# Four chunks convolved ahead of the expert units, the other stages spread between them

## The chip, the cores and the metric

The kernel runs on one core of one Trainium2 chip. The metric is the device time of one execution in microseconds. Three runs of the kernel before gave 195.55, 196.88 and 197.39 us, median 196.88 us.

## The reference, cut to what matters

The input is 32 images of 64 channels and 16x16 pixels. A first layernorm over channels (LN1) is followed by a blockwise fp4 quantisation, a 3x3 convolution with quantised weights and a residual. Then each pixel is a token of 64 values: a second layernorm (LN2), a gate that picks two of eight experts, and the experts themselves, all eight computed for every token and weighed by the gate (zero for the experts not picked).

```python
x = x + conv(fake_quant(_ln_c(x)), fake_quant(w))        # fake_quant: 16 values share a power-of-two scale
xf = _ln_t(to_tokens(x))
probs = softmax(xf @ gate_w + gate_b);  cw = the top two of probs, zero elsewhere
for e in range(8):
    out += cw[:, e] * (gelu(xf @ W1[e] + b1[e]) @ W2[e] + b2[e])      # 64 -> 128 -> 64
x = x + from_tokens(out)
```

## The kernel before

**Tiles.** The 16 pairs of images lie as [128, 4096]: 2 x 64 channels on the partitions, pixels on the free axis. They are cut into NCH = 8 chunks of W = 512 columns. A chunk is 1024 tokens.

**Stages of a chunk.** LN1: TensorE centres (`center_chunk`, a product with a centring matrix, which also turns the tile), ScalarE squares, VectorE sums (`reduce_squares`), ScalarE takes the root (`deviations`), VectorE inverts and multiplies (`invert`, `normalise`; ScalarE does it for chunks 6 and 7). Quantisation: TensorE turns the chunk back (`transpose_xn`), ScalarE takes the absolute value (`take_v`), VectorE finds the maxima of blocks and rounds by adding and removing a large number (`block_maxima`, `block_bounds`, `block_magics`, `magics`, `bias`), GpSimd writes the result as bf16 into a padded tile (`quantised`). Convolution: nine products of 128x512 (`convolve`), residual (`take_conv` on ScalarE and `residual` on GpSimd, or `residual` on VectorE for chunks 5 to 7). LN2 goes as LN1 (`center_x2`, `square`, `reduce_squares`, `deviations`, `invert`, `normalise`), then the fp32 values are split in two fp16 halves (`high_half`, `low_half`), turned (`transpose_halves`) and copied out of PSUM (`take_xT`). Routing: TensorE makes the logits (`logits`), VectorE shifts them by their maximum (`shifted_logits`), ScalarE takes exponentials, VectorE finds the two largest and their places (`route_max`, `route_index`) and computes the weights (`route_select`, `route_gates`); TensorE turns them (`transpose_gates`), ScalarE copies them (`take_gateT`), and SyncE writes them to DRAM and reads them back spread over all partitions into `gbc` (`spread_gates`, 2 MB a chunk in four transfers, each awaited by the first unit that needs it).

**Expert units.** One chunk times one expert is a unit n = 8c + u; there are 64. `first_product` is eight fp16 matmuls of 128x512 (two halves of W1, two column groups, two image sets) into one of two pairs of PSUM banks; `gelus` is one ScalarE instruction on 128x1024; `second_product` is four fp32 matmuls; `weigh` on VectorE adds the bias and multiplies by the spread gate; `add_unit` on GpSimd adds to x2. `first_product(n)` waits for the gelu of n-2, `second_product(n)` for the gelu of n and the weighing of n-2, `weigh(n)` for the addition of n-4. On TensorE the order is first product of n, second product of n-2.

**Order.** Every engine runs its own queue in program order, written out by hand, and waits on semaphores. In the kernel before, all eight chunks go through LN1, quantisation, convolution, residual and nearly all of LN2 first. Four chunks are turned and have logits, and chunk 0 has its gates, when TensorE issues `ffn(0, first=True)`; the halves and logits of chunks 4 to 7 stand between the units of chunk 0. From chunk 1 on each block of eight units holds only the routing of a later chunk: on VectorE `route_gates(c + 2)` stands after `weigh` of unit 4 of chunk c, on TensorE `transpose_gates(c + 1)` after unit 1 of chunk c. ScalarE, GpSimd, VectorE and SyncE run this part in loops, TensorE unrolled. Exponentials are taken in three lots (`LOGIT_PARTS`), so the Gelu table of ScalarE is loaded twice (L563, L567). The end (L922 to L924): VectorE adds the last unit itself, then the last chunk is stored.

## Time and profile before

| what | value |
|---|---|
| median of three runs | 196.88 us |
| the profiled execution | 198.83 us |
| its span, first to last instruction | 195.9 us |
| TensorE (PE) matmuls busy | 166.7 us, 85% of the span |
| VectorE (DVE) busy | 138.3 us, 71% |
| GpSimd (POOL) busy | 127.9 us, 65% |
| ScalarE (ACT) busy | 116.7 us, 60% |
| mean granted TensorE clock | 0.952 |

The profiled execution lies 1.95 us above the median of the runs, and 2.9 us of it lie outside the span. All times in rows are microseconds from the start of the span unless marked ns. A matmul's end is modelled, and matmuls overlap, so the pace is read from start to start and not from the length of one.

### The profile page before, as it was taken

Reading aid. Unit: us, or ns where it says so; the run is one execution under the profiler, and the core shown is the slowest. Engines: PE = TensorE matmul, PEld = TensorE weight load, DVE = VectorE, ACT = ScalarE, POOL = GpSimd, SP = SyncE. Lnnn points to the kernel's source line nnn. Section 1 sums busy time; section 2 is a strip of 40 time slices with the busy share of each in tenths; the row PEclk is TensorE's granted clock in tenths of the full one; section 3 lists DMA queues with packets and bytes.
Section 4 is the critical chain, followed back from the end, with each engine's and each line's share of the span. In section 5 each row is a group of like instructions: output and inputs, shape, how many; then the busy total and the mean of one; then the engine's idle time right before and its main releaser. Section 6 shows DMA issues by size and latency. Waiting matters only on the chain.

```text
span 195.9 us, 3972 instructions
## 1 busy us (share of the span) xinstructions
PE 166.7 (85%) x1214; PEld 84.6 (43%) x1214; DVE 138.3 (71%) x442; ACT 116.7 (60%) x153; POOL 127.9 (65%) x120
## 2 busy tenths in 40 slices
PE   1986159899773697997999999999999899999980
PEld 1984125465472343542443443444443344444420
DVE  0899999999778985794684784595694395344451
ACT  3276902572488283469776767766776656776630
POOL 7699134799980442457577677577668477588482
PEclk9999859999997579999999999999999999999998
DMA  6990000000000059499089379569469559669601
GB/s 163 326 134 0 3 0 2 3 0 3 0 0 0 10 161 206 77 215 199 17 204 206 83 168 208 117 169 207 116 158 201 133 149 208 136 159 204 172 0 54
DMA packets 16320, 22.39 MB, mean 114 GB/s; under 512 B 2344, under 2 KB 8112, under 8 KB 16304
## 3 DMA queue, kind: packets, MB, share of 16 engines
q1 hardware_dynamic: 16144, 22.04, 50.3%
q8 instruction: 9, 0.15, 0.3%
q10 hardware_dynamic: 160, 0.15, 0.3%
q14 instruction: 7, 0.06, 0.1%
HBM read 19.82 MB, written 2.36 MB: 113 GB/s over the span
## 4 chain that ended last, share of the span: by engine, by line
PE 48%; DVE 25%; DMA 11%; ACT 7%; issue 6%; SPq 1%; POOLq 1%; ACTq 0%; DVEq 0%
PE ps L1060 23%; PE ps L1077 21%; DMA gbc<-gate_rows 6%; DVE xn L721 5%; DVE ssum L629 4%; DVE xn L641 2%; DMA gate_rows<-gateT 2%; DVE gbc L703 2%; DMA cw<-in_conv_w 2%; ACT xn L458 2%; DVE gbc L708 1%; DVE gbc L713 1%; PE ps L1016 1%; ACT hl L504 1%; DVE topi L801 1%
## 5 line engine op out<-in xcount | busy, mean ns | idle before, releaser
L411 POOL TENSOR_TENSOR x<-x,y_sb 128x512 f32 (+1 forms) x63 | 80.3, 1274 | 40.7 <-DVE y_sb L840 36.5
L557 ACT ACTIVATE work<-ps,bias_sb,w_back 128x1024 f32<-128x1024 f32 x64 | 77.0, 1204 | 37.9 <-PE ps L1060 37.7
L840 DVE SCALAR_TENSOR_TENSOR y_sb<-ps,bias_sb,gbc 128x512 f32<-128x512 f32 x64 | 47.4, 746 | 41.4 <-PE ps L1077 29.6
L1077 PE MATMUL ps<-work,w_sb 128*64 128x512 f32 x256 | 65.7, 593 | 1.0 <-DVE y_sb L840 0.9
L1060 PE MATMUL ps<-xT,w_hi 128*64 128x512 f16 x256 | 39.6, 389 | 1.1 <-ACT work L557 1.1
L1060 PE MATMUL ps<-xT,w_lo 128*64 128x512 f16 x256 | 39.3, 387 | 0.0
L1060 PEld LDWEIGHTS ps<-xT,w_hi 128*64 128x64 f16 x256 | 13.7, 111 | 33.3 <-issue 30.5
L1077 PEld LDWEIGHTS ps<-work,w_sb 128*64 128x64 f32 x256 | 17.9, 137 | 14.1 <-issue 2.1
L1060 PEld LDWEIGHTS ps<-xT,w_lo 128*64 128x64 f16 x256 | 15.0, 112 | 13.5 <-issue 1.0
L983 PE MATMUL ps<-qpad,cw_bd 128*128 128x512 bf16 x72 | 19.0, 411 | 1.7 <-POOL qpad L355 1.6
L355 POOL TENSOR_TENSOR qpad<-work,xn 128x512 bf16<-128x512 f32 (+1 forms) x8 | 10.6, 1328 | 8.7 <-DVE work L727 8.7
L390 POOL TENSOR_TENSOR hl<-xn,hl x8 | 9.2, 1160 | 9.1 <-DVE hl L763 9.0
L430 ACT ACTIVATE work<-ps 128x512 f32<-128x512 f32 x16 | 9.5, 594 | 7.4 <-PE ps L936 7.4
L936 PE MATMUL ps<-center,x_sb 128*128 128x128 f32 x64 | 10.1, 336 | 4.1 <-DMA x_sb<-in_x 4.1
L629 DVE TENSOR_REDUCE ssum<-work 128x8 f32<-128x512 f32 x16 | 10.4, 678 | 2.6 <-ACT work L430 2.6
L936 PEld LDWEIGHTS ps<-center,x_sb 128*128 128x128 f32 x64 | 9.9, 251 | 4.0 <-POOL stack_id L323 4.0
L983 PEld LDWEIGHTS ps<-qpad,cw_bd 128*128 128x128 bf16 x72 | 7.0, 102 | 10.2 <-issue 3.6
L451 ACT ACTIVATE work<-ps 128x512 f32<-128x512 f32 x8 | 4.6, 633 | 8.6 <-PE ps L950 8.6
L721 DVE SCALAR_TENSOR_TENSOR xn<-work,gbc 128x512 f32<-128x512 f32 x8 | 9.6, 1202 | 0.0
L641 DVE TENSOR_TENSOR xn<-ps,rstd 128x512 f32<-128x512 f32 x14 | 9.2, 681 | 0.1
L936 PE MATMUL ps<-center,x 128*128 128x128 f32 x64 | 8.6, 278 | 0.6 <-POOL x L363 0.6
L936 PEld LDWEIGHTS ps<-center,x 128*128 128x128 f32 x64 | 8.2, 191 | 1.9 <-POOL x L363 1.1
(113 smaller groups left out, 175.8 us busy)
## 6 DMA issues: line engine op xcount, KB each, us to landing
gbc<-gate_rows SPq DMA_DIRECT2D x16, 768.0 KB, 10.1
gbc<-gate_rows SPq DMA_DIRECT2D x16, 256.0 KB, 4.0
x_sb<-in_x SPq DMA_DIRECT2D x8, 256.0 KB, 5.3
out<-x SPq DMA_DIRECT2D x8, 256.0 KB, 10.4
w_raw<-in_W SPq DMA_DIRECT2D x2, 256.0 KB, 6.5
w_sb<-in_W SPq DMA_DIRECT2D x1, 256.0 KB
gate_rows<-gateT SPq DMA_DIRECT2D x8, 32.0 KB, 3.8
cw<-in_conv_w ACTq DMA_DIRECT2D x2, 72.0 KB, 3.9
```

The lines of the kernel that those rows point to most:

```text
L355: pool.tensor_tensor(qpad[:, ds(2 * c, 2), 1:SIDE + 1, 1:SIDE + 1], work[:, ds(c * W, W)].rearrange("p (q h w) -> p q h w", q=2, h=SIDE), ...
L411: pool.tensor_tensor(x2[:, ds(c * W, W)], x2[:, ds(c * W, W)], y_sb[:, u % H_RING, :], ALU.add).then_inc(added, 1)
L430: act.activation(work[:, ds(c * W, W)], bank(c), ACT.Square).then_inc(squared, 1)
L557: act.activation(h_sb[:, u % H_RING, :], bank(H + 2 * (u % 2), 2 * W), ACT.Gelu, bias=b1_sb[:, u:u + 1], scale=w_back[:, u:u + 1]).then_in ...
L629: dve.tensor_reduce(ssum[:, ds(c, 1), :].rearrange("p z g -> p (z g)"), by_group(work[:, ds(c * W, W)]), AX.X, ALU.add).then_inc(summed, 1)
L641: dve.tensor_tensor(by_group(xn[:, ds(c * W, W)]), by_group(bank(c)), wide_groups(rstd, c), ALU.mult).then_inc(ready, 1)
L721: dve.scalar_tensor_tensor(blk(xn[:, ds(c * W, W)]), blk(work[:, ds(c * W, W)]), MAGIC, smallest.to_broadcast([128, BLKS, BLK]), ALU.mult, ...
L840: dve.scalar_tensor_tensor(y_sb[:, u % H_RING, :], bank(Y + u % 2), b2_sb[:, u:u + 1], gbc[:, slot, u, :], ALU.add, ALU.mult).then_inc(wei ...
L936: last = pe.matmul(ps[:, col:col + 128], src[:, col:col + 128], center[:, :], start=True, stop=True)
L983: last = pe.matmul(bank(c), cw_bd[:, k, :, :].rearrange("p r o -> p (r o)"), qpad[:, ds(2 * c, 2), k // 3:k // 3 + SIDE, k % 3:k % 3 + SID ...
L1060: last = pe.matmul(ps[q * CH:(q + 1) * CH, at:at + W], w_half[:, u * HIDDEN + q * CH:u * HIDDEN + (q + 1) * CH], xT[:, ds(c * CTOK + r * W ...
L1077: last = pe.matmul(ps[r * CH:(r + 1) * CH, (Y + u % 2) * W:(Y + u % 2 + 1) * W], w2_sb[:, u, :], h_sb[:, u % H_RING, r * W:(r + 1) * W], s ...
```

## The change

The work of each stage is nearly the same. Its place in the five queues is another.

- **In front** of unit 0 stand: LN1 of all chunks; quantisation, convolution and residual of chunks 0 to 3 (`HEAD = 4`); LN2, halves, turning and logits of chunks 0 and 1; the routing of chunk 0.
- **All else** stands in one loop over s = 0 ... 65 on each engine, unrolled. In step s TensorE issues the first product of unit s, the second product of unit s-2, and then what `due` names: a stage with distance `ahead` is issued for chunk c in step s = 8c - ahead. ScalarE issues the due stages and then the gelu of s, VectorE the due stages and then `weigh(s - 2)`, GpSimd the due stages and then `add_unit(s - 3)`.
- The distances are constants at the top: turning 29, absolute value 28, maxima and bounds 27, magics 26, bias 25, quantised 24, convolution 23, residual 21, centring 17, squares 16, sums 15, root 14, normalise 13, high half 12, low half and turning of halves 11, copy 10, logits 9, shift 8, maxima of logits 7, index and exponentials 6, gates and turning of gates 4, copy of gates 3.
- Banks 0 and 1 of PSUM serve all stages in the loop; each TensorE stage waits until the one before has been read.
- Exponentials are taken per chunk, each followed by a load of the Gelu table. The root of LN2 of chunks 2 to 7 is a power of -0.5 on GpSimd.
- `route_copy` goes. Residual is VectorE's for all chunks, high half ScalarE's for all. The convolution weights are spread by one VectorE and one ScalarE instruction in place of four VectorE ones, and their scale is multiplied into the sign on VectorE in place of a GpSimd step.
- `gbc` is filled in eight transfers of 256 KB a chunk in place of two of 256 KB and two of 768 KB, each part awaited by the unit that first needs it, and each written once the weighing two chunks before is past it.
- `h_sb` is a tile of its own.

```diff
+LN1_PARTS = ((0, 3), (3, 8))
+HEAD = 4
+GATE_PARTS = ((0, 2), (2, 4), (4, 6), (6, 8))
+TURN, ABS, BOUND, MAGN, BIASED, QUANT, CONV, RESID = 29, 28, 27, 26, 25, 24, 23, 21
+CENTRE, SQUARE, SUMS, ROOT, NORM, HIGH, LOW, TURNH, TAKEN, LOGITS = 17, 16, 15, 14, 13, 12, 11, 11, 10, 9
+SHIFT, TOPS, EXPS, INDEX, GATES, TURNG, TAKENG = 8, 7, 6, 6, 4, 4, 3
+        def due(s, ahead):
+            c, rest = divmod(s + ahead, UNITS)
+            return c if rest == 0 and c < NCH else None
...
@@ sync @@
+                    if c >= 2:
+                        sp.wait_ge(weighted, UNITS * (c - 2) + last)
...
+            for c in range(NCH):
+                send_rows(c)
+                spread_gates(c)
+                if c >= 2:
+                    store(c - 2)
...
@@ gpsimd @@
+            quantised(0)
+            quantised(1)
+            pool.wait_ge(w_inv_ready, 1)
+            pool.tensor_tensor(by_expert(w_scaled), by_expert(w_raw), ...
+            quantised(2)
+            pool.wait_ge(w_hi_ready, 1)
             pool.tensor_tensor(w_lo[:, :], w_scaled[:, :], w_hi[:, :], ALU.subtract).then_inc(w_lo_ready, 1)
+            low_half(0)
+            quantised(3)
+            low_half(1)
+            for s in range(SLOTS + 2):
+                for ahead, stage in ((QUANT, quantised), (ROOT, inverse_root), (LOW, low_half)):
+                    c = due(s, ahead)
+                    if c is not None and not (stage is quantised and c < HEAD):
+                        stage(c)
+                if 3 <= s:
+                    add_unit(s - 3)
...
@@ scalar @@
+            deviations2(1)
+            high_half(1)
+            load_table(ACT.Exp)
+            exponentials(0)
+            load_table(ACT.Gelu)
+            take_xT(1)
+            for s in range(SLOTS):
+                for ahead, stage in ((HIGH, high_half), (ABS, take_v), (SQUARE, square2),
+                                     (TAKEN, take_xT), (EXPS, exponentials), (TAKENG, take_gateT)):
+                    c = due(s, ahead)
+                    if c is not None:
+                        stage(c)
+                        if stage is exponentials:
+                            load_table(ACT.Gelu)
+                gelu(s)
+                if s == 0:
+                    take_gateT(0)
...
@@ vector @@
+            reduce1(0)
+            upper_steps()
+            reduce1(1) ... reduce1(3); invert1(0); normalise1(0); reduce1(4); normalise1(1); reduce1(5) ... reduce1(7)
+            bounds(0); invert1(1); normalise1(6); normalise1(7); spread_conv_weights()
+            magics(0); bias(0); take_conv_weights(); normalise1(2); weight_maxima()
+            bounds(1); magics(1); bias(1); weight_exponents(); residual(0); normalise1(3); weight_powers()
+            bounds(2); magics(2); bias(2); reduce2(0); residual(1); invert2(0); normalise2(0)
+            bounds(3); magics(3); bias(3); reduce2(1); residual(2); invert2(1); normalise2(1)
+            shifted_logits(0); settled(); route_max(0); route_index(0); residual(3); route_gates(0)
+            for s in range(SLOTS + 2):
+                for ahead, stage in ((SHIFT, shifted_logits), (SUMS, reduce2), (TOPS, route_max), (INDEX, route_index),
+                                     (NORM, normalise2), (RESID, residual), (GATES, route_gates),
+                                     (BOUND, bounds), (MAGN, magics), (BIASED, bias)):
+                    c = due(s, ahead)
+                    if c is not None and not (stage is residual and c < HEAD):
+                        stage(c)
+                if s == 3:
+                    weigh(0)
+                    weigh(1)
+                if s >= 4:
+                    weigh(s - 2)
...
@@ tensor @@
+            def first_product(n):
+                c, u = divmod(n, UNITS)
+                pe.wait_ge(xT_ready, c + 1)
+                if n < 2:
+                    pe.wait_ge(x2_by_dve, HEAD)
+                    pe.wait_ge(xn1_by_act, len(LN1_ACT))
                 else:
                     pe.wait_ge(gelu_done, n - 1)
...
+            convolve(3)
+            turn_halves(1)
+            centre2(2)
+            logits(1)
+            for s in range(SLOTS + G2_LAG):
+                if s < SLOTS:
+                    first_product(s)
+                if s >= G2_LAG:
+                    second_product(s - G2_LAG)
+                if s == 0:
+                    turn_gates(0)
+                for ahead, stage in ((CONV, convolve), (TURN, turn_chunk), (TURNG, turn_gates), (TURNH, turn_halves),
+                                     (LOGITS, logits), (CENTRE, centre2)):
+                    c = due(s, ahead)
+                    if c is not None and not (stage is convolve and c < HEAD):
+                        stage(c)
```

On VectorE the lines with several calls stand for one call a line. `route_gates(c)` now holds both comparisons of the places, the sum of the exponentials, its reciprocal, the sum of the two selections, the pick and the last product.

## Rows read from the trace of the kernel before

**Rows 1.** Windows: stretch and its length; busy time (instructions) of each engine; clock; DMA

```profile
9.10:57.00 47.90, 37.29 (x239) 25.06 (x238) 46.27 (x89) 25.01 (x62) 35.94 (x30) 0.93 0.12 18
66.00:71.50 5.50, 5.50 (x33) 2.44 (x32) 5.07 (x18) 3.66 (x6) 3.47 (x3) 0.52 0.21 69
106.00:190.00 84.00, 83.01 (x564) 34.64 (x563) 50.58 (x176) 56.42 (x52) 59.53 (x48) 1.00 0.69 155
```

The engines stand in the order PE, PEld, DVE, ACT, POOL.

**Rows 2.** Chain that ended last: start, us, what (L1060 first product, L1077 second)

```profile
66.29 1.85 PE ps L1060 x6
...
77.41 0.55 PE ps L1016 x8
...
78.95 0.86 PE ps L1077 x4
79.81 0.89 PE ps L1029 x32
...
95.40 0.86 PE ps L1060 x8
96.27 0.86 PE ps L1077 x4
...
189.18 1.09 PE ps L1077 x4
...
190.30 0.76 DVE y_sb L840
```

L1016 turns halves, L1029 makes logits (here of two chunks).

**Rows 3.** Timeline of PE: start, us, engine, line (L950 turn, L983 conv, L936 centre)

```profile
33.52 0.60 PE L950 MATMUL ps<-identf,xn 128*128 128x128 f32 x4
33.95 2.19 PE L983 MATMUL ps<-qpad,cw_bd 128*128 128x512 bf16 x9
...
40.86 2.19 PE L983 MATMUL ps<-qpad,cw_bd 128*128 128x512 bf16 x9
42.89 1.05 PE L936 MATMUL ps<-center,x 128*128 128x128 f32 x8
43.77 1.05 PE L983 MATMUL ps<-qpad,cw_bd 128*128 128x512 bf16 x4
```

**Rows 4.** Groups of instructions by line and shape: busy us, mean ns, idle before

```profile
L708 DVE TENSOR_SCALAR gbc<-gbc 128x32 f32<-128x32 f32 x8 | 3.5, 439 | 0.0
...
L504 ACT ACTIVATE hl<-xn 128x512 f16<-128x512 f32 x4 | 2.5, 630 | 2.5 <-DVE xn L641 2.5
...
L511 ACT ACTIVATE xT<-ps 128x1024 f16<-128x1024 f16 x4 | 4.0, 1020 | 0.0
```

**Rows 5.** Timeline in front: sums, two largest logits, then the spreading of chunk 0's gates

```profile
11.20 1.86 DVE L629 TENSOR_REDUCE ssum<-work 128x8 f32<-128x512 f32 x3
...
61.08 0.58 DVE L795 MAX8 top<-lcur 128x8 f32<-128x8 f32 x8
...
66.33 0.27 ACT L526 ACTIVATE gateT<-ps 64x128 f32<-64x128 f32 x1 [2.63 <-PE ps L1045]
...
76.21 0.74 DVE L840 SCALAR_TENSOR_TENSOR y_sb<-ps,bias_sb,gbc 128x512 f32<-128x512 f32 x1
```

**Rows 6.** Timeline of DVE and POOL around the gates of one chunk

```profile
115.63 1.27 POOL L411 TENSOR_TENSOR x<-x,y_sb 128x512 f32 x1 [0.34 <-DVE y_sb L840]
...
115.73 1.25 DVE L823 TENSOR_TENSOR picked<-ex,sel 128x64 f32<-128x64 f32 x1
...
117.02 0.27 DVE L827 TENSOR_TENSOR gate<-picked,rsum 128x64 f32<-128x64 f32 x1
```

**Rows 7.** Timeline around the exponentials of chunks 4 to 7 and the next first product

```profile
87.40 1.28 ACT L518 ACT_TABLE_LOAD   x1
88.69 0.42 ACT L518 ACTIVATE ex<-ex 128x256 f32<-128x256 f32 x1
...
90.53 3.62 ACT L557 ACTIVATE work<-ps,bias_sb,w_back 128x1024 f32<-128x1024 f32 x3
...
91.77 0.62 PE L1060 MATMUL ps<-xT,w_hi 128*64 128x512 f16 x4 [1.11 <-ACT work L557]
```

More of the change, by code:

```diff
@@ new lines, in gelu @@
+            def gelu(n):
+                act.wait_ge(g1_done, n + 1)
+                if n >= H_RING:
+                    act.wait_ge(g2_done, n - H_RING + 1)
+                u = n % UNITS
+                act.activation(h_sb[:, n % H_RING, :], bank(H + 2 * (n % 2), 2 * W), ACT.Gelu,
+                               bias=b1_sb[:, u:u + 1], scale=w_back[:, u:u + 1]).then_inc(gelu_done, 1)
+            act.wait_ge(eps_ready, 1)
+            load_table(ACT.Sqrt)
+            for c in range(5):
+                square1(c)
@@ L652, in _, with reduce1, invert1 @@
-            normalise(3, LN1_PARTS, rstd1, xn1_ready)
-            invert(LN1_PARTS, 1, std1, rstd1)
-            for c in range(4, XN_BY_DVE):
-                normalise(c, LN1_PARTS, rstd1, xn1_ready)
+                return t[:, c, :].unsqueeze(2).to_broadcast([128, GROUPS, CH])
+            def reduce1(c):
+                dve.wait_ge(sq1, c + 1)
+                dve.tensor_reduce(ssum[:, c, :], by_group(chunk(work, c)), AX.X, ALU.add).then_inc(ss1, 1)
+            def invert1(k):
+                first, last = LN1_PARTS[k]
+                dve.wait_ge(std1_ready, k + 1)
+                dve.reciprocal(rstd[:, first:last, :], std[:, first:last, :]).then_inc(rstd1, 1)
@@ new lines, in _ @@
+            normalise1(0)
+            reduce1(4)
+            normalise1(1)
+            reduce1(5)
+            reduce1(6)
+            reduce1(7)
+            bounds(0)
+            invert1(1)
+            normalise1(6)
+            normalise1(7)
+            spread_conv_weights()
+            magics(0)
+            bias(0)
+            take_conv_weights()
+            normalise1(2)
+            weight_maxima()
+            bounds(1)
+            magics(1)
+            bias(1)
+            weight_exponents()
@@ L880, in _ @@
+            residual(0)
+            normalise1(3)
+            weight_powers()
+            bounds(2)
+            magics(2)
+            bias(2)
+            reduce2(0)
+            residual(1)
+            invert2(0)
+            normalise2(0)
+            bounds(3)
+            magics(3)
+            bias(3)
+            reduce2(1)
+            residual(2)
+            invert2(1)
+            normalise2(1)
             shifted_logits(0)
             settled()
-            route_copy(0)
-            invert(LN2_PARTS, 2, std2, rstd2)
@@ new lines, in _ @@
+            last.then_inc(bT_ready, 1)
+            pe.wait_ge(cwx_by_dve, 1)
+            pe.wait_ge(cwx_by_act, 1)
+            for k in range(TAPS):
+                last = pe.matmul(ps[:, TAPS_AT + k * CH:TAPS_AT + (k + 1) * CH],
+                                 cw_x[:, k, :, :, :].rearrange("p a b c -> p (a b c)"),
+                                 stack_id[:, :], start=True, stop=True)
+            last.then_inc(cwT_ready, 1)
+            pe.wait_ge(cwbd_by_act, 1)
+            pe.wait_ge(cwbd_by_dve, 1)
@@ L1106, in _ @@
+            convolve(2)
+            centre2(1)
+            turn_halves(0)
             pe.wait_ge(w_lo_ready, 1)
[L1107 removed]
             logits(0)
+            convolve(3)
+            turn_halves(1)
+            centre2(2)
             logits(1)
[L1110 to L1117 removed]
```

838 lines of the change are left out of this document (304 added, 534 removed).

## The prediction

> **What bounds the kernel now.** I read the windows first. Between 9.1 and 57 us VectorE is busy 46.3 of 47.9 us, TensorE 37.3; between 106 and 190 us TensorE is busy 83.0 of 84.0 us and no other engine over 60 [rows 1]. So there are two kernels in one: a front bound by VectorE, and units bound by TensorE. The chain of waits says the same: from 92 us to 190 it alternates between first and second product, 0.86 us each, so a unit is 1.72 us and 64 of them 110 us [rows 2]. The first product of unit 0 starts at 66.3 us, at a granted clock of 0.52 of full speed, close to the lower level of 1.2 GHz [rows 1, 2]. The second product of unit 2 starts at 78.95, the last one at 189.18, and 6.7 us later the span of 195.9 us ends [rows 2].
>
> The profiled execution is 198.83 us: its span and 2.9 us around it. It stands 1.95 above the median of 196.88. I work out a new span and put the difference on the median.
>
> **The question.** The change takes VectorE's work out of the front, but puts TensorE's share of it into the stretch where TensorE has 1 us of slack in 84. I compare the moment of the second product of unit 2 (from there on the units run) and what TensorE has left after it.
>
> **The front.** VectorE's queue sets it. Before, 46.3 us of work stand between 9.1 and 57 [rows 1], with 52 instructions on 128x512 (15 sums, 10 normalisations, 8 each of maxima, magics, biases, 3 residuals). The new queue has 34 up to `residual(3)`. In a row each takes 0.62 us, three sums being 1.86 [rows 5]: 18 fewer are 11.2 us less. Of the small bounds 8 go, 0.4 each with their waits for GpSimd [rows 4]: 3.2 less. Routing of chunk 0 comes in: three dependent steps of 0.3, the maxima 0.6 [rows 5], their places, 8 pairs of instructions that I take at 1.2, twice the maxima: 2.7 more. The sign product adds 0.5. Sum 35.1. To this I add 1.6 of waiting: VectorE issues `weight_exponents` before `residual(0)`, behind a product that TensorE issues after the convolution of chunk 0 (about 1.0), and `reduce2(1)` waits for the centring behind the convolution of chunk 2 (0.6). `residual(3)` ends at 9.2 + 35.1 + 1.6 = 45.9.
>
> But unit 0 waits for more: TensorE issues `logits(1)` ahead of it. `normalise2(1)` ends 3.3 us before `residual(3)` (2.7 of routing, 0.6 of the residual), at 42.6. Then ScalarE: high half 0.63 [rows 4], the Exp table, the exponentials and the Gelu table, 3.1 us from 87.40 to 90.53 before [rows 7], the copy 1.02 [rows 4]; then logits 0.45, half of 0.89 [rows 2]; handing over 0.2. Together 5.4: the first product of unit 0 starts at **48.0**, 18.3 earlier. It takes 1.85 at the low clock [rows 2], the gelu before `take_gateT(0)` 1.2 and a hand-over 0.15: the gates' copy starts at 51.2. From that copy to the first weighing were 9.9 us, all of it the two transfers [rows 5]. The first weighing starts at 61.1, the second product of unit 2 at 61.1 + 0.8 = **61.9**, against 78.95: 17.05 us gained.
>
> **What TensorE has left after that moment.** Before: 189.18 - 78.95 = 110.2 us. Of this 1.2 was the wait for ScalarE's tables: the first product at 91.77 follows the late gelu [rows 7], where it was due at about 90.6. 1.0 was idle between 106 and 190 [rows 1], which I take to be late gates and to vanish with the smaller transfers. So 108.0 of work. The loop adds, at full clock and from start to start [rows 3]: four convolutions of 42.89 - 40.86 = 2.03 (8.1); three turnings of 0.43 (1.3; the fourth stands before the moment); five centrings of 43.77 - 42.89 = 0.88 (4.4); six turnings of halves, 0.5 between the 0.55 in the loop [rows 2] and the 0.44 of logits, which have as many passes (3.0); two logits more than the four before (0.9); one turning of gates more (0.3). Sum 18.0. **Without any wait the change gives back what it gains: 17.05 against 18.0 - 2.2 = 15.8.** The rest depends on waits.
>
> **A wait in the same step.** `TURNG` and `GATES` are both 4: TensorE turns the gates in the step in which VectorE computes them. A weighing starts 1.1 us after its second product [rows 2], so 2.0 after the step's first product, and takes 0.7. VectorE's stages of step s stand behind `weigh(s - 3)`, so they start 2.0 + 0.7 - 1.7 = 1.0 us into step s. For chunks 2 to 5 the step before carries `normalise2` and `residual`, 1.2 us, and with TensorE's longer step that makes 0.85 (chunks 2 to 4) or 1.3 (chunk 5). `route_gates` now holds everything from the comparisons on. Unhindered it is 1.4. But GpSimd starts adding as soon as the weighing is done, and in the loop one of VectorE's small products then takes 1.25 in place of 0.22 and ends with GpSimd's instruction [rows 6]. In the new order that addition starts some 0.2 after the gates begin, released by the weighing right before them, and lasts 1.27 [rows 6]; after it three small products are left, 0.7. I take 2.2 for the step. TensorE is there 1.72 into its step. It waits 0.85 + 2.2 - 1.72 = 1.35 for chunks 2, 3, 4; 1.8 for chunk 5; 1.45 for chunks 6 and 7: 8.75. For chunk 1 the gates stand behind `weigh(0)` and `weigh(1)`, which wait for the transfers: 2.0. Sum 10.8. Behind the wait stands the next first product, so TensorE loses all of it. Bounds: 0.5 each, unhindered (3.5), to 2.3 each, if two additions stand in the way (16). I take the middle, since the one addition is what the row shows.
>
> **Tables.** Exponentials per chunk cost ScalarE two loads: from the gelu's end to the next gelu's start about 3.0 us for 64 columns. Where a convolution precedes, TensorE's step is 3.75 long, and the gelu comes 0.3 late, within its slack of 1.0: no cost, and it is the convolution that covers it. Chunks 6 and 7 have no convolution before: 1.2 each as before [rows 7], 2.4. Chunk 1's lies under the wait for the first gates. The exponential starts the moment its load ends, 87.40 + 1.28 against 88.69 [rows 7]. The Trainium skill ("ScalarE: Activation LUTs", What ACT_TABLE_LOAD costs) counts a drain of 1.38 us on top of each load; by that the step would cost 2.8 more, some 2 us of TensorE at four chunks and 4 at two, the sum 14 to 16 us worse. The trace disagrees: no gap stands there.
>
> The other pairs close in time (turning against `normalise2`, centring against `bias`) come out 0.1 to 0.4 us early for TensorE and cost nothing; if VectorE is later by 0.5 they cost as much, 4 times each. GpSimd's `pow` on 128x8 is not in the trace: from 0.1 (the row's smallest kind) to 1.3, one addition; I take 0.3. It has over 4 us before `normalise2` needs it, and GpSimd is busy 59.5 of 84 us [rows 1], so both ends cost nothing. Unrolled queues may gain the loops' few register steps or stall on code; neither shows, 0 to 3 us.
>
> **Sum.** 61.9 + 108.0 + 18.0 + 10.8 + 2.4 = 201.1 for the last second product, + 6.7 for the unchanged end = 207.8. Against 195.9 that is +11.9: median **208.8 us**. In short: waits of 1.6 (front), 10.8 and 2.4 stand on a sum that would else be close to no change.
>
> **Rivals.** *The waits don't come (faster).* Place: VectorE's and TensorE's step 8c - 4, and the front. If VectorE's front runs with fewer waits for GpSimd, 4 us earlier, and the gates are always ready when TensorE comes, the sum is 207.8 - 4 - 10.8 = 193.0, median 194.0, and without the tables' 2.4 it is 191.6. For it: before, VectorE's front holds magics stretched by GpSimd, and fewer GpSimd steps stand in the new front. Against: rows 6 shows the wait in the loop. It decides when 14 us less are waited than in my sum. Chance 0.22, of which 0.20 faster by over 1%.
> *Half of it.* The gates cost 0.5 to 1 each (3.5 to 7 in place of 10.8), the front is up to 2 shorter, the tables cost 0 to 2.4: span 196 to 202, median 197 to 203. 0.24, half of it no change.
> *Late gates (slower still).* From the turned gates of chunk 7 to its first weighing there are 10.6 us (five steps of 1.72 and 2.0), and the first spreading took 9.9 [rows 5]. If a part lands 2 us later, each of chunks 5 to 7 stalls 1 to 2: +4 to +6, 213 to 215. Chance 0.09.
> *The front isn't shortened*: if ScalarE or GpSimd holds it so that unit 0 starts at 55 or later, +7: 216. 0.04.
> My forecast, 203 to 213, keeps 0.41.
>
> **Numbers.** A difference of 1%, 2 us, is about what a measurement of this kernel tells from none. Faster 0.20, same 0.14, slower 0.66. The forecast's own range is 203 to 213. Some 13 in a hundred lie below 193 and 6 above 215, so the range is 193 to 215.
>
> **What would show each step.** First product of unit 0 at 48.0, first weighing at 61.1, second product of unit 2 at 61.9; TensorE waiting for VectorE's gate product seven times for 1.3 to 2.0 us; two first products late by 1.2 behind the tables of chunks 6 and 7; conv in the loop 2.03 from start to start. I am wrong if the gate waits are under 0.5, or if unit 0 starts before 44.

## The result, and the profile of the changed kernel

| | median of the runs, us | ratio to before [95%] | profiled execution, us | its span, us |
|---|---|---|---|---|
| before | 197.13 (195.55 to 197.92, 4 runs) | | 198.83 | 195.9 |
| changed | 216.34 (214.60 to 217.75, 4 runs) | 1.0988 [1.0924, 1.1053] | 215.84 | 214.0 |

The change makes the kernel 9.9% slower: 19.2 us between the medians, 18.1 between the spans. I had forecast 208.8 in a range of 193 to 215. The direction was right. The size was not: 11.9 us expected, and the time lies above the range. Ratios, here and below, are taken over the undisturbed executions alone (now and then one comes out over 1.5% longer than the fastest of its kernel), so they need not be the quotient of the medians beside them.

The windows of the changed kernel come first (columns as in [rows 1]: stretch, length, busy time and instructions of PE, PEld, DVE, ACT, POOL, then clock and DMA).

```profile
9.10:57.00 47.90, 35.68 (x225) 21.76 (x224) 39.84 (x126) 28.62 (x62) 22.29 (x20) 0.79 0.11 19
61.00:65.00 4.00, 1.98 (x4) 0.32 (x4) 3.90 (x9) 0.00 (x0) 3.60 (x3) 0.50 1.07 238
65.00:72.00 7.00, 6.82 (x33) 2.82 (x35) 3.62 (x7) 2.81 (x4) 2.91 (x2) 0.56 0.53 125
```

In the first line VectorE is busy 39.8 of 47.9 us in place of 46.3 [rows 1], and from 49.9 us on the window holds units already. The next two lines are the start of the units. TensorE is busy 2 of 4 us there, and for 11 us it works at 0.50 to 0.56 of full speed. That low stretch also existed before, at 66 to 71.5 us [rows 1].

The chain of waits shows how the units start (start, us, what), and answers to [rows 2]:

```profile
49.98 1.00 PE ps L927 x8
...
52.40 2.97 DMA gate_rows<-gateT
...
56.05 3.99 DMA gbc<-gate_rows
60.13 1.41 DVE y_sb L760 x2
...
63.74 1.09 DVE picked L746
```

L927 is the first product, L941 the second. The first product of unit 0 stands at 49.98, then the two transfers of chunk 0's gates follow, the first weighing at 60.13, and right behind it the gates of chunk 1. TensorE waits for these gates.

Waits of TensorE, summed over the span (waiting, releaser: us, times, longest); those left out lie ahead of unit 2:

```profile
PE ps L912 <- DVE gate L749: 10.2, 6, 2.2
...
PE ps L927 <- ACT h_sb L483: 3.9, 4, 1.3
...
PE ps L941 <- DVE y_sb L760: 2.2, 1, 2.2
```

L912 turns the gates, L749 is their product on VectorE: this is the wait I had forecast at 10.8 us. The chunks repeat every 8 units, so one period shows the loop. This is TensorE between 98 and 110 us, with the waits in brackets (answers to [rows 3]; L869 convolution, L859 turning):

```profile
98.27 0.60 PE L927 MATMUL ps<-xT,w_hi 128*64 128x512 f16 x4
...
100.09 2.20 PE L869 MATMUL ps<-qpad,cw_bd 128*128 128x512 bf16 x9
102.22 0.62 PE L927 MATMUL ps<-xT,w_hi 128*64 128x512 f16 x4
...
103.97 0.60 PE L927 MATMUL ps<-xT,w_hi 128*64 128x512 f16 x4
...
105.79 0.66 PE L859 MATMUL ps<-identf,xn 128*128 128x128 f32 x4
106.38 0.62 PE L927 MATMUL ps<-xT,w_hi 128*64 128x512 f16 x4
...
109.75 0.30 PE L912 MATMUL ps<-identf,gate 128*64 128x128 f32 x1 [1.46 <-DVE gate L749]
109.97 0.62 PE L927 MATMUL ps<-xT,w_hi 128*64 128x512 f16 x4
```

A unit alone takes 1.72 us [rows 2]. The step that holds the convolution takes 102.22 - 98.27 = 3.95, so the convolution costs 2.23 there. The step with the turning takes 106.38 - 103.97 = 2.41, so it costs 0.69. I had 2.03 and 0.43 from the front [rows 3]. In the last step the gates come 1.46 late.

Below, **the interval** is the time from one chunk's turned gates to the next chunk's, eight units long (13.76 us of products alone, 8 x 1.72). It is read from the timeline of TensorE, and it is where the experiments are compared:

| kernel | gates 0 turned at | intervals 0-1, 1-2, ... 6-7 |
|---|---|---|
| changed | 50.9 | 14.28, 23.67, 20.90, 20.88, 20.88, 19.38, 16.87 |
| changed, run again | | 14.23, 23.22, 20.89, 20.89, 20.89, 20.94, 16.86 |
| gates a step earlier | 49.6 | 11.19, 20.05, 19.74, 19.75, 19.11, 18.85, 17.29 |
| earlier from chunk 2 | | 14.65, 21.57, 19.74, 19.74, 19.11, 18.86, 17.28 |
| earlier for chunk 1 | | 10.71, 21.94, 20.89, 20.89, 20.89, 19.37, 16.87 |
| no tables in the loop | | 14.52, 23.20, 20.89, 20.89, 20.88, 20.94, 18.28 |
| one tap | | 13.77, 20.75, 19.36, 19.38, 19.37, 19.36, 16.87 |
| small additions | | 12.46, 21.91, 20.08, 20.08, 20.08, 17.86, 16.86 |
| both first gates sooner | 48.8 | 10.17, 19.86, 19.59, 19.59, 19.59, 17.86, 16.86 |
| full-width product | | 13.12, 23.12, 21.48, 21.48, 21.48, 19.64, 17.63 |
| half-width product | | 15.36, 23.10, 21.07, 21.07, 21.07, 21.11, 17.02 |

Interval 5-6 has two values, 19.4 and 20.9, in kernels that wait 2.16 us for chunk 5's gates. In the changed kernel run again (and without tables, and with the half-width product) TensorE's clock falls about 1 us behind that wait and stays low for some 3 us, and a second product lasts 1.91 us in place of 1.02:

```profile
150.59 1.91 PE L941 MATMUL ps<-h_sb,w_sb 128*64 128x512 f32 x4
...
151.60:153.60 2.00, 2.00 (x14) 0.95 (x12) 0.75 (x1) 0.53 (x2) 0.21 (x1) 0.50 0.01 1
```

In the first execution of the changed kernel, and with only chunk 1's gates earlier, the wait is the same and the clock stays at 1.00. This low stretch costs 1.5 us in some executions and is missing in others. That the wait brings it on is inferred from its place.

### The profile page after: what moved, and what is told of

Read it like the earlier page. It is cut to its first block, busy times and chain, and to the rows that moved or that the text cites. A ratio compares the mean times of both kernels' runs of the same rounds, so it can differ in the third digit from the quotient of the medians.

```text
span 214.0 us, 3702 instructions
## 1 busy us (share of the span) xinstructions
PE 177.1 (83%) x1214; PEld 85.3 (40%) x1214; DVE 145.6 (68%) x444; ACT 138.3 (65%) x179; POOL 130.9 (61%) x127
## 4 chain that ended last, share of the span: by engine, by line
PE 58%; DVE 25%; DMA 5%; ACT 5%; issue 4%; POOL 1%; POOLq 1%; SPq 0%; ACTq 0%; DVEq 0%
PE ps L927 22%; PE ps L941 19%; PE ps L869 8%; PE ps L838 3%; DVE picked L746 3%; DVE y_sb L760 3%; DVE sel L745 2%; DVE ssum L598 2%; DMA cw<-in_conv_w 2%; DVE xn L628 2%; DMA gbc<-gate_rows 2%; PE ps L891 2%; PE ps L901 2%; ACT L414 2%; DVE x L709 1%
## 5 line engine op out<-in xcount | busy, mean ns | idle before, releaser
L381 POOL TENSOR_TENSOR x<-x,y_sb 128x512 f32<-128x512 f32 x63 | 81.9, 1300 | 54.0 <-DVE y_sb L760 53.5
L483 ACT ACTIVATE h_sb<-ps,bias_sb,w_back 128x1024 f32<-128x1024 f32 x64 | 76.7, 1203 | 24.0 <-PE ps L927 23.9
L941 PE MATMUL ps<-h_sb,w_sb 128*64 128x512 f32 x256 | 67.4, 607 | 2.3 <-DVE y_sb L760 2.2
L927 PE MATMUL ps<-xT,w_hi 128*64 128x512 f16 x256 | 40.0, 392 | 3.9 <-ACT h_sb L483 3.9
L927 PE MATMUL ps<-xT,w_lo 128*64 128x512 f16 x256 | 39.0, 384 | 0.0
L869 PE MATMUL ps<-qpad,cw_bd 128*128 128x512 bf16 x72 | 22.7, 473 | 2.6 <-POOL qpad L356 2.6
L941 PEld LDWEIGHTS ps<-h_sb,w_sb 128*64 128x64 f32 x256 | 18.3, 139 | 15.1 <-ACT h_sb L483 3.6
L927 PEld LDWEIGHTS ps<-xT,w_hi 128*64 128x64 f16 x256 | 12.0, 110 | 30.3 <-issue 26.9
L927 PEld LDWEIGHTS ps<-xT,w_lo 128*64 128x64 f16 x256 | 15.0, 112 | 13.4 <-issue 1.0
L356 POOL TENSOR_TENSOR qpad<-work,xn 128x512 bf16<-128x512 f32 x8 | 10.2, 1274 | 11.5 <-DVE work L704 11.5
L869 PEld LDWEIGHTS ps<-qpad,cw_bd 128*128 128x128 bf16 x72 | 7.7, 113 | 16.5 <-issue 11.4
L912 PE MATMUL ps<-identf,gate 128*64 128x128 f32 x8 | 2.5, 315 | 10.2 <-DVE gate L749 10.2
L425 ACT ACTIVATE work<-ps 128x512 f32<-128x512 f32 x8 | 4.8, 598 | 9.4 <-PE ps L838 9.4
L371 POOL TENSOR_TENSOR hl<-xn,hl 128x512 f16<-128x512 f32 x8 | 9.2, 1153 | 2.1 <-ACT hl L456 2.1
L462 ACT ACTIVATE xT<-ps 128x1024 f16<-128x1024 f16 x8 | 8.2, 1022 | 3.3 <-PE ps L891 3.3
L366 POOL TENSOR_TENSOR rstd<-std,power 128x8 f32<-128x8 f32 x6 | 9.9, 1652 | 0.5
```

The costliest lines, as they stand in the source:

```text
L356: pool.tensor_tensor(qpad[:, 2 * c:2 * c + 2, 1:SIDE + 1, 1:SIDE + 1], chunk(work, c).rearrange("p (q h w) -> p q h w", q=2, h=SIDE), chun ...
L366: pool.tensor_tensor(rstd2[:, c, :], std2[:, c, :], power[:, :], ALU.pow).then_inc(rstd2_by_pool, 1)
L371: pool.tensor_tensor(hl[:, c, :, 1, :].rearrange("p (r t) c -> p t r c", r=2), chunk(xn, c).rearrange("p (t r c) -> p t r c", r=2, c=CH), ...
L381: pool.tensor_tensor(chunk(x2, c), chunk(x2, c), y_sb[:, n % H_RING, :], ALU.add).then_inc(added, 1)
L462: act.activation(xT[:, c * CTOK:(c + 1) * CTOK], bank(S0 if c == 0 else S1).bitcast(fp16), ACT.Copy).then_inc(xT_ready, 1)
L483: act.activation(h_sb[:, n % H_RING, :], bank(H + 2 * (n % 2), 2 * W), ACT.Gelu, bias=b1_sb[:, u:u + 1], scale=w_back[:, u:u + 1]).then_in ...
```

## The experiments

**My theory** after the result: the gate wait in the step (10.2 us) and the start of the units at a low clock explain what can be undone. The rest is the plain price of TensorE's stages between units, which is higher than I had it. **The rivals:** the tables' loads are the true bound, with the gate wait only showing in front of them; or the convolutions cost far more than their 2.2 us. The kernels of a group ran on one chip and are compared with runs of the kernel before on it (medians of all of these: 199.09, 198.47 and 199.86 us). Where spans are compared with the changed kernel, its first profiled execution (214.0) is meant unless the repeat (213.6) is named.

### Gates one step earlier, for all chunks and for a part of them

```
-TURN, ABS, BOUND, MAGN, BIASED, QUANT, CONV, RESID = 29, 28, 27, 26, 25, 24, 23, 21
+TURN, ABS, BOUND, MAGN, BIASED, QUANT, CONV, RESID = 29, 28, 27, 26, 25, 24, 23, 22
-SHIFT, TOPS, EXPS, INDEX, GATES, TURNG, TAKENG = 8, 7, 6, 6, 4, 4, 3
+SHIFT, TOPS, EXPS, INDEX, GATES, TURNG, TAKENG = 8, 7, 6, 6, 5, 4, 3
```

> The changed kernel with VectorE's gates one step earlier (GATES 5, for every chunk from 1 on) and its residual one step earlier to make room (RESID 22); TensorE turns the gates where it did. Theory A (TensorE waits because both stand in the same step): the waits of TensorE for the gates' last product, 10.2 us in the profile of the changed kernel, go to under 1 us; some of the low clock after the first wait goes too. Span 200 to 203, median about 204. Theory B (VectorE is short of time in the loop, so the wait moves on to weighings or centrings): the gates' wait goes, but at least 6 us of new waits for VectorE appear and the median stays above 211.

Measured: 203.68 us, ratio 1.0225 [1.0141, 1.0309], span 201.9, so 12.1 us of span less than the changed kernel. No wait of TensorE for gates is left. The two tables' stalls of 1.27 us stay, and so does this one of the loop:

```profile
PE ps L891 <- POOL hl L371: 2.6, 6, 0.9
```

L891 is the turning of halves, which waits for GpSimd's low half. So the gates, once out of the way, leave a second and smaller wait. The windows of the start answer to those above:

```profile
61.00:65.00 4.00, 4.00 (x29) 1.78 (x30) 3.93 (x6) 2.23 (x3) 3.22 (x4) 0.83 0.68 148
65.00:72.00 7.00, 7.00 (x64) 3.63 (x62) 3.99 (x9) 4.45 (x5) 5.04 (x5) 1.00 0.74 179
```

TensorE is busy all the time and the clock is at 1.00 from 65 us. The second interval falls from 23.67 to 20.05. Its later neighbours fall only from 20.9 to 19.7, so I put some 2.5 us of this fall down to the clock.

Two kernels split the move. In the first, chunk 1 keeps its old place and only chunks 2 to 7 go earlier. In the second, only chunk 1 goes earlier (`RESID` stays). Both issue `route_gates` at one of two distances by the chunk's number:

```
+                    if stage is route_gates and c is not None and (ahead == GATES) != (c >= 2):
+                        continue
```

> As the run before, but chunk 1's gates stay in their old step. Theory A: only the six waits from chunk 2 on go, 8.0 us: median 208, span 206. The wait of 2.2 for chunk 1 and the low clock behind it stay. Theory B: above 213.

Measured: 208.54 us, 1.0465 [1.0374, 1.0555], span 206.7. One wait for gates is left:

```profile
PE ps L914 <- DVE gate L749: 2.2, 1, 2.2
```

> The changed kernel with only chunk 1's gates a step earlier, ahead of the first weighings. Theory A: 2.2 us of waiting go, and TensorE's low clock between 61 and 71 us ends sooner; together 3 to 5 us: median 212 to 213. If the clock were no part of it, 2.2 alone: 214.

Measured: 210.21 us, 1.0580 [1.0474, 1.0687], span 207.7, and of the waits for gates 8.0 us in 5 remain (`c < 2` in place of `c >= 2` in the edit).

Chunks 2 to 7 alone give 7.3 us of span, about their 8.0 of waits. Chunk 1 alone gives 6.3, where its own wait is 2.2. Not all of this is the stall's price: the first weighing stands at 58.09 here, at 60.13 in the changed kernel and at 58.53 in its repeat, so 2.0 of the 6.3 lie ahead of it, where two executions of one kernel differ by 1.6. From the first weighing to chunk 2's turned gates there are 24.4 us here, against 28.7 and 28.3. So the stall of 2.2 us costs about 4, nearly twice its length, because TensorE then goes on at the low clock. Together the two kernels give 13.6 and the full move 12.1, so they overlap a little. I had expected 212 to 213 for the second one, and underrated this.

### No table loads in the loop

```
-... ACT.Exp).then_inc(exp_ready, 1)
+... ACT.Exp if c == 0 else ACT.Copy).then_inc(exp_ready, 1)
...
-                        if stage is exponentials:
-                            load_table(ACT.Gelu)
```

The exponentials of chunks 1 to 7 are replaced by a copy, so no table changes after the start.

> The changed kernel with a copy in place of the exponential for chunks 1 to 7, and no loads of tables in the loop: it leaves out the exponentials. Theory A: the loads cost TensorE only where no convolution stands before, chunks 6 and 7, 1.27 each, and chunk 7's gates then have to be waited for, 1.4: median 1 to 2.5 below the changed kernel, 214 to 215. Rival (every one of the seven pairs of loads costs, 2.6 each or more): 18 us less, under 200.

Measured: 217.24 us, 1.0904 [1.0810, 1.0998], span 215.5. Nothing was gained, where I had expected 2 us. The waits for gates grew instead:

```profile
PE ps L910 <- DVE gate L747: 12.8, 7, 2.9
```

They rose by 2.6 us, and there is one more of them. The two stalls of 1.27 behind the tables are gone, and the gates are waited for in their place: interval 6-7 even rose from 16.87 to 18.28, as behind the wait of 2.9 us for chunk 6's gates the clock is at 0.50 from 172 to 174 us. The tables' rival is out: they are not the bound as long as the gates are late in the same period. A stall that lies ahead of a wait in the same queue cost nothing by itself here. What the tables cost once the gates are in time no run shows.

### Convolutions of the loop with one tap in nine

```
-                for k in range(TAPS):
+                taps = range(TAPS) if c < HEAD else range(1)
+                for k in taps:
```

The convolutions of chunks 4 to 7 leave out eight of nine taps.

> The changed kernel with one product of nine in the convolutions of chunks 4 to 7, those in the loop: it leaves out eight taps of them. Theory A (TensorE's own work sets the loop, and a convolution covers ScalarE's tables): 32 products of 0.213 us go, 6.8 us, but four first products then stand 1.2 us behind the tables as those of chunks 6 and 7 do now: 2 to 3 us less in all, 213 to 214. If the tables needed no cover: 6.8 less, 209. If other engines set the loop: no change.

Measured: 207.32 us, 1.0513 [1.0221, 1.0805], span 205.7, which is 8.9 us below the run of the changed kernel on the same chip, where I had expected about 3. TensorE's timeline, at chunk 3's period and at chunk 5's:

```profile
101.13 0.62 PE L928 MATMUL ps<-xT,w_hi 128*64 128x512 f16 x4 [0.24 <-ACT h_sb L483]
...
139.88 0.62 PE L928 MATMUL ps<-xT,w_hi 128*64 128x512 f16 x4 [0.83 <-ACT h_sb L483]
```

I had held that the convolution covers the table loads, so that without it each period would wait 1.2 us more. The wait is 0.24 at chunks 2 to 4, where a turning stands in a step between (100.24 us), and 0.83 at chunk 5, where none does; with nine taps it is nothing at all four. So either stage covers a part of the loads. The interval fell from 20.89 to 19.37, so 1.52 of the 1.81 us that eight taps take came back. That is 6.1 us over four intervals. The rest is the start (intervals 0-1 and 1-2 give 1.4 more) and interval 5-6, where the run of the changed kernel on this chip has the low clock and this one has not (1.6). The step "it is the convolution that covers it" in my prediction was therefore incomplete in its reason, and right in its price of almost nothing. That the convolutions cost much more than 2.2 us each is ruled out.

### Small additions on GpSimd

```
-... pool.tensor_tensor(chunk(x2, c), chunk(x2, c), y_sb[:, n % H_RING, :], ALU.add)
+... pool.tensor_tensor(chunk(x2, c)[:, 0:8], chunk(x2, c)[:, 0:8], y_sb[:, n % H_RING, 0:8], ALU.add)
```

GpSimd adds 8 of 512 columns of each unit's output. The question is whether GpSimd stretches VectorE's small products.

> The changed kernel with GpSimd adding only 8 of the 512 columns of each unit: it leaves out the rest of the addition. Order and waits are as they were. Theory A (VectorE's small products of the gates stand behind GpSimd's addition): route_gates takes 1.4 us in place of 3.0, the gates' wait on TensorE falls from 10.2 to under 2 us, and the low clock behind the first goes in part: median 203 to 206. Rival (the gates are late because of their place alone): the wait stays above 7 us and the median above 212.

Measured: 207.06 us, 1.0540 [1.0369, 1.0711], span 204.6. The gates' wait fell from 10.2 to 4.0, where I had expected less than 2 (and a median of 203 to 206):

```profile
PE ps L912 <- DVE gate L749: 4.0, 5, 1.4
```

In the changed kernel VectorE and GpSimd stand like this around the gates of a chunk (it answers to [rows 6]):

```profile
106.70 0.22 DVE L739 TENSOR_TENSOR sel<-iota_e,topi 128x64 f32<-128x64 f32 x1
...
107.34 0.93 DVE L745 TENSOR_TENSOR sel<-sel 128x64 f32<-128x64 f32 x1
108.31 1.07 DVE L746 TENSOR_TENSOR picked<-ex,sel 128x64 f32<-128x64 f32 x1
109.42 0.27 DVE L749 TENSOR_TENSOR gate<-picked,rsum 128x64 f32<-128x64 f32 x1
```

```profile
106.87 1.32 POOL L381 TENSOR_TENSOR x<-x,y_sb 128x512 f32<-128x512 f32 x1 [0.57 <-DVE y_sb L760]
108.15 1.15 POOL L371 TENSOR_TENSOR hl<-xn,hl 128x512 f16<-128x512 f32 x1
```

GpSimd's addition ends at 108.19 and VectorE's product of L745 at 108.27. GpSimd's low half ends at 109.30 and the product of L746 at 109.38. Two products in a row, each 0.17 to 0.23 us where GpSimd does nothing beside them, end with the GpSimd instruction beside them. With the small addition one of the two is free; the other, beside the low half (102.37 to 103.52), is not:

```profile
102.63 0.97 DVE L745 TENSOR_TENSOR sel<-sel 128x64 f32<-128x64 f32 x1
103.64 0.22 DVE L746 TENSOR_TENSOR picked<-ex,sel 128x64 f32<-128x64 f32 x1
```

`route_gates` takes 2.2 us there against 3.0 in the changed kernel. The Trainium skill ("SBUF — State Buffer", Who interferes with whom) describes this as a lock: a VectorE operation with two inputs in SBUF and a GpSimd operation that reads SBUF exclude each other. The trace agrees, with 0.22 against 0.93 and 1.07 us.

### Both first gates sooner

```
-... HIGH, LOW, TURNH, ... = 17, 16, 15, 14, 13, 12, 11, 11, 10, 9
+... HIGH, LOW, TURNH, ... = 17, 16, 15, 14, 13, 12, 12, 11, 10, 9
+            turn_gates(0)
             logits(1)
...
             take_xT(1)
+            take_gateT(0)
```

This stands on top of the gates a step earlier: the low half also goes a step earlier, chunk 0's gates are turned before chunk 1's logits, and ScalarE copies them before the first gelu. The old calls inside slot 0 go out.

> Version meant to be faster: gates and residual a step earlier as in e1, low halves a step earlier (LOW 12), and chunk 0's gates turned ahead of logits(1) and copied ahead of the first gelu. Against e1, 203.7: the 2.6 us that TensorE waited for low halves go, and the first weighing comes 1.2 to 2 us sooner: 199 to 201. Still not below the kernel before, since TensorE's work in the loop stays what it is.

Measured: 200.22 us, 1.0173 [1.0018, 1.0328], span 198.6. That is 15.4 us of span less than the changed kernel, and the clock stays at 1.00 from unit 0 to the end of the units. It is still not faster than before. The waits for gates that are left:

```profile
PE ps L911 <- DVE gate L748: 2.0, 5, 0.9
```

One of these, 0.7, stands ahead of unit 0; 1.3 are in the loop, and so are the two tables' stalls.

This is the most telling run on my sum. I had worked out that without any wait the change gives back what it gains: 17.05 against 15.8 us. Here the second product of unit 2 starts at 57.9, so the front gives 21.0, four more than I had. From there TensorE has 134.6 us to its last second product. Less 1.3 for gates and 2.5 for tables that is 130.8 of work, where my sum has 108.0 + 18.0 = 126.0. No low clock is in it, so the added stages cost 22.8 in place of 18.0. This eats what the front gives, and the span is 2.7 above that of the kernel before.

### What a change of width costs TensorE

My loop stages cost 0.2 us each more than in the front. The candidate is the change between products of 128 and of 64 rows (128\*128 and 128\*64 in the timeline), since in the front products of full width follow each other. In two kernels a tiny product of 8 columns stands ahead of every first product from unit 2 on, once full and once half as wide. The first product writes over what it leaves.

```
+                if n >= 2:
+                    pe.matmul(ps[:, (H + 2 * (n % 2)) * W:(H + 2 * (n % 2)) * W + EXPERTS],
+                              xT[:, c * CTOK:c * CTOK + 128], w_hi[:, NW:NW + EXPERTS], start=True, stop=True)
```

> The changed kernel with one tiny product more ahead of each first product from unit 2 on: 8 columns, 128 weights columns wide like those of the stages, while first and second products are 64 wide. Its result is overwritten. Theory A (each change between a stage and the units costs TensorE 0.15 to 0.25 us of its own, which my sum left out): 62 changes more, of which those beside a stage or in a wait cost nothing; where a chunk has two plain boundaries and four with a stage, the period between two turnings of gates grows by 1 us or more: median 5 to 12 above the changed kernel's 216.2, 221 to 228. Rival (the extra time in the loop is waits, not changes): under 2 us, median below 218.

Measured: 218.78 us, 1.1089 [1.1010, 1.1169], span 216.7. Against the changed kernel's 213.6 in the repeat that is +3.1 of span. It lies between what I had expected if changes of width cost (221 at least) and if they don't (below 218), so I go by the steps. The plain step (two products, nothing between; PEld are loads of weights) shows the price:

```profile
190.26 0.62 PE L930 MATMUL ps<-xT,w_hi 128*64 128x512 f16 x4
...
192.10 0.10 PEld L924 LDWEIGHTS ps<-w_hi,xT 128*128 128x128 f16 x1 [0.81 <-issue]
192.11 0.18 PE L924 MATMUL ps<-w_hi,xT 128*128 128x8 f16 x1
192.21 0.14 PEld L930 LDWEIGHTS ps<-xT,w_hi 128*64 128x64 f16 x4
192.22 0.62 PE L930 MATMUL ps<-xT,w_hi 128*64 128x512 f16 x4
```

From 190.26 to 192.22 are 1.96 us in place of 1.72: +0.24. The steps that hold a stage of full width hardly grow: convolution 3.95 to 3.98, turning 2.41 to 2.44, centring with logits 3.31 to 3.34, turning of halves 2.40 to 2.40. So one more product of full width costs 0.2 where none stands and next to nothing where one does: these steps had paid for the change already. In the loop's period the total rose by 0.59 only, three plain steps of 0.2 and little else.

> The same tiny product, but with 64 columns of weights like the units' own, so that the width doesn't change. If the cost of a stage between units lies in the change of width: under 2 us above the changed kernel. If any product of another kind costs the same: as much as with the full width.

The same with 64 rows (`ps[0:CH, ...]`, and 64 columns of `xT`). Measured: 216.40 us (213.74 to 217.98), 1.0864 [1.0722, 1.1007]. Its profiled execution is the longest of the four, so I read only the plain step, at full clock (chain first: start, us, what; then the timeline):

```profile
191.74 0.90 PE ps L930 x8
...
193.49 0.90 PE ps L930 x8
```

```profile
192.90 0.11 PEld L924 LDWEIGHTS ps<-w_hi,xT 128*64 128x64 f16 x1
...
193.33 0.17 PE L924 MATMUL ps<-w_hi,xT 128*64 128x8 f16 x1
```

It takes 1.75 us: +0.03. The same instruction at half the width costs an eighth, so the price belongs to the full width between half widths. The loads show where it arises: at equal width the weights are loaded 0.43 us ahead of their product (192.90 for 193.33), at a change of width only with it, on the way over (192.10) and back (192.21). The loop's stages in the changed kernel have the same sign. The load for a plain step stands 0.43 ahead (103.54 for 103.97), that of the turning and that behind it do not:

```profile
103.54 0.11 PEld L927 LDWEIGHTS ps<-xT,w_hi 128*64 128x64 f16 x2 [0.29 <-issue]
...
105.78 0.42 PEld L859 LDWEIGHTS ps<-identf,xn 128*128 128x128 f32 x4 [0.81 <-issue]
...
106.37 0.14 PEld L927 LDWEIGHTS ps<-xT,w_hi 128*64 128x64 f16 x4 [0.17 <-issue]
```

In the front of the kernel before, a turning stands behind a convolution, which is as wide, and its load 0.22 ahead of its product at 33.52 [rows 3]:

```profile
33.30 0.57 PEld L950 LDWEIGHTS ps<-identf,xn 128*128 128x128 f32 x4
```

The Trainium skill ("TensorEngine Tiling (Array Packing)", Key Properties) says that changing the tiling mode drains TensorE. The trace agrees, as no load is made ahead across a change, and the figure here is 0.2 us for going over and back. My prediction did not weigh this rule.

### The changed kernel again

> The changed kernel itself, once more, to have it on the same chip as the next three: median near 216, TensorE waiting 10.2 us for the gates.

Measured: 216.22 us, 1.1009 [1.0808, 1.1210], span 213.6, again with 10.2 us of waits for gates. The first product of unit 0 stands at 48.45 in it and the first weighing at 58.53, so the front moves by 1.5 us from execution to execution while the end moves by 0.4. What the front gains here is lost in interval 5-6 (20.94 against 19.38), to the low clock behind chunk 5's gates.

### The kernel before, with its gates spread in four parts

```
-GATE_PARTS = ((0, 2), (2, 8))
+GATE_PARTS = ((0, 2), (2, 4), (4, 6), (6, 8))
```

Each part gets its own semaphore. Everything else is the kernel before. It tests my assumption that the 1.0 us of idle time between 106 and 190 [rows 1] is late gates.

> The kernel before with one part of the change alone: the gates spread in eight transfers of 256 KB a chunk, each quarter awaited by its own unit. My sum let 1.0 us of waiting for late gates vanish with it: the stall before 157 us goes, span 195, 0.5 to 1% faster than before. Rival: the second wait in that place moves to the second quarter, no difference.

Measured: 195.92 us (195.13 to 196.41, 12 runs), ratio 0.9924 [0.9894, 0.9954], span 194.6. The window in question first before, then here:

```profile
150.00:160.00 10.00, 9.10 (x66) 3.91 (x64) 6.07 (x35) 6.53 (x7) 5.68 (x5) 1.00 0.58 140
```

```profile
150.00:160.00 10.00, 10.00 (x72) 4.25 (x70) 7.05 (x36) 7.36 (x7) 7.52 (x6) 1.00 0.56 144
```

The wait for the large second part is gone: VectorE's weighings waited 11.6 us in 6 for `gbc` before, and the profile shows no such wait now. The gain is 0.8%, and it is the only version measured here that is faster than the kernel before. The other parts of the change were not tried on it one by one.

## Why the prediction was right in direction and wrong in size

| step | forecast, us | measured, us |
|---|---|---|
| first product of unit 0 | 48.0 | 49.9 (48.4 in the repeat) |
| chunk 0's gates copied, to first weighing | 9.9 | 8.0 |
| second product of unit 2 | 61.9 | 61.0 (59.4 in the repeat) |
| waits for gates | 10.8, in 7 | 10.2, in 6 |
| waits behind tables | 2.4, in 2 | 2.5, in 2 |
| TensorE's rest from unit 2 to the last second product | 108.0 + 18.0 = 126.0 | 147.0 - 10.2 - 2.5 = 134.3 |
| after the last second product | 6.7 | 5.9 |

**The step that failed** is "Sum 18.0", TensorE's added stages, which I priced "at full clock and from start to start" by rows of the front. It fell short by 8.3 us:

- *Changes of width, about 4.1.* From the timeline of one period, each step less 1.72: convolution 2.23 against 2.03, turning 0.69 against 0.43, a turning of halves 0.68 against 0.5, centring with logits 1.59 against 1.33, gates 0.41 against 0.3. By their number (4, 3, 6, 5 and 1 new) that is 0.8, 0.8, 1.1, 1.3 and 0.1 us. The two tiny products show that a change of width costs this much, and that the steps with a stage had paid it. The rows of the front that I used had full-width neighbours, and a sign stood in my rows: the turning of halves is 0.55 in the loop and logits with as many passes 0.44 [rows 2], which I averaged where I should have asked why.
- *The low clock, about 3.8.* Before, the low stretch, 66 to 71.5 us [rows 1], lay ahead of unit 2's second product, so the 108.0 has none of it. In the changed kernel it lies behind that moment, and there I priced it nowhere. TensorE stands for 2.19 us before the second product of unit 2 and for 2.18 before chunk 1's gates, and works at 0.50 to 0.56 until 71.5. Interval 1-2 is 23.67 where later ones are 20.9, so 2.8 more, and the second product of unit 2 alone lasts 1.98 in place of 1.02, so 1.0 more:

```profile
61.02 1.98 PE L941 MATMUL ps<-h_sb,w_sb 128*64 128x512 f32 x4 [2.19 <-DVE y_sb L760]
...
65.18 0.42 PE L912 MATMUL ps<-identf,gate 128*64 128x128 f32 x1 [2.18 <-DVE gate L749]
```

  The 1.0 costs no time by itself, since TensorE then stands until the gates come at 65.18 in any case. With the full-width product the clock is still high at this place: the second product takes 1.08 and the wait is 3.08. Moving the gates of chunk 1 alone shows the price of the stretch: about 4 us for a wait of 2.2. With both first gates sooner it doesn't occur, and interval 1-2 is 19.86 against 19.59 later. TensorE's work is 130.8 there against 134.3, 3.5 less.
- *About 0.4* I can't place.

On the median the miss is 7.5 us: 6.2 are the spans (7.0 at the last second product, less 0.8 at the end), and 1.3 come from scaling by one profiled execution, since before's stood 1.95 above its median and 2.9 above its span, and that of the changed kernel 0.5 below and 1.8 above.

**The front** was right within 1 us at the moment that counts, in the first execution, and by luck. Unit 0 came 1.9 later, its first product ran at full clock (1.0 where I had 1.85), and the transfers were 1.9 shorter. In the repeat the moment is 59.4, 2.5 earlier than my 61.9. I had the low clock ahead of the units, where it cost 0.85 in my sum. It came behind unit 2, where my sum has nothing.

**The wait in the same step** was right in place and sum and nearly in number (six of seven), and the move of `GATES` by one step shows it. The sum is partly luck: chunk 1's wait would be 1 us longer, had TensorE not been slow ahead of it. Inside it two more terms were off. I took 2.2 us for `route_gates`, with one product behind GpSimd's addition; it takes 3.0, because the low half right behind that addition catches a second one. And VectorE's stages ahead of it end earlier than I had it, and chunk 7 doesn't wait, as its gates stand behind the tables' stall.

**Tables** cost two stalls of 1.27 as forecast, at the two chunks without a convolution:

```profile
167.53 0.62 PE L927 MATMUL ps<-xT,w_hi 128*64 128x512 f16 x4 [1.27 <-ACT h_sb L483]
...
185.92 0.62 PE L927 MATMUL ps<-xT,w_hi 128*64 128x512 f16 x4 [1.27 <-ACT h_sb L483]
```

But taking them out brings nothing, since the gates' wait takes their place, so "10.8 and 2.4" were no sum of independent prices. At the other chunks convolution and turning cover them. The exponential still starts the moment the load ends, so the drain of 1.38 us behind each load that the Trainium skill counts ("ScalarE: Activation LUTs", What ACT_TABLE_LOAD costs) doesn't stand here either:

```profile
100.57 1.28 ACT L468 ACT_TABLE_LOAD   x1
101.86 0.26 ACT L468 ACTIVATE ex<-ex 128x64 f32<-128x64 f32 x1
```

**Late gates vanish with smaller transfers** was right, shown on the kernel before itself. **The power on GpSimd** takes 1.65 us, above my upper bound of 1.3. The one wait for it is VectorE's, 0.2 us at chunk 2, so it costs nothing, as forecast:

```profile
L366 POOL TENSOR_TENSOR rstd<-std,power 128x8 f32<-128x8 f32 x6 | 9.9, 1652 | 0.5
```

**The rivals.** That the waits don't come is refuted by the trace. The version with both first gates sooner is close to what that rival described, a front 4 us earlier and gates nearly always ready, for which I had worked out a span of 193.0. Its front is 4.0 earlier, and its span is 198.6: 4.8 more for the stages and 1.3 for gates that still come late, less 0.7 at the end. So that rival rested on the same 18.0. With 18.0 + 4.1 - 2.2 = 19.9 given back for 17.05 gained, the change loses 2.9 even without waits and with the front as I had it.

## What to carry to other kernels

Price a stage that is moved between other work by what it does to the step it goes into, not by its length among its own kind: here every change from half to full width and back cost TensorE about 0.2 us, and over all the added stages that turned 1.2 us gained into 2.9 lost. A stage and its consumer in the same step of a pipeline meant a wait at six of seven chunks here, and a place one step earlier is the first thing to try (12 us). Where the engine that bounds the kernel stalls while its clock is low, count more than the stall (here about 4 us for 2.2).

## What the runs showed that I had not expected

- A product of 8 columns at full width between products of half width adds 0.24 us to the step, at half width 0.03. The weights of a product are loaded 0.43 us ahead of it at equal width, and only with it where the width changes.
- GpSimd's power on 128x8 takes 1.65 us, more than an addition on 128x512 (1.32).
- Two small products of VectorE in a row can each be held by a GpSimd instruction (0.93 and 1.07 in place of 0.22), when GpSimd issues two right behind each other.
- A stall of 2.2 us at the start of the units costs about 4, since TensorE goes on at the lower of its two clock levels (1.2 GHz, 0.50 to 0.56 of full speed in the windows) for some 10 us.
- In the middle of the loop the same wait of 2.16 us is followed by some 3 us at the low clock in one execution of the kernel and by none in another, a difference of 1.5 us.
